# Fetching fifteen of 416 gathered edge tiles row by row from two other queues, in a graph network kernel

## The reference, cut to what matters

```
h = (x @ W).reshape(n, 8, 32)
a_src, a_dst = einsum(h, att_src), einsum(h, att_dst)        # [n, 8]
e = leaky_relu(a_src[src] + a_dst[dst], 0.2)                 # per edge and head
e = exp(e - segment_max(e, dst)[dst])
alpha = e / (segment_sum(e, dst)[dst] + 1e-16)
out = segment_sum(h[src] * alpha, dst) + bias                # then layernorm, residual, layernorm
```

## Time and profile before

| | |
|---|---|
| median of three runs | 2902.57 us |
| the profiled execution's own time | 2898.8 us |
| its span, first to last instruction | 2896.7 us |
| mean granted clock of TensorE | 0.877 |
| TensorE, matmul busy | 2220.1 us (77%) |
| VectorE busy | 1490.0 us (51%) |
| GpSimd busy | 1216.4 us (42%) |
| ScalarE busy | 663.0 us (23%) |

### The profile page before, as it was taken

How to read it: one execution, slowest core, us unless ns; L and a number is a source line. 1 busy time by engine, 2 the same in 40 slices (tenths; PEclk the granted TensorE clock), 3 DMA queues, 4 the chain that set the end, 5 groups by cost and what they waited for, 6 DMA issues and landing times.

```text
span 2896.7 us, 31032 instructions
## 1 busy us (share of the span) xinstructions
PE 2220.1 (77%) x8708; PEld 1498.8 (52%) x8708; DVE 1490.0 (51%) x4063; ACT 663.0 (23%) x1371; POOL 1216.4 (42%) x1733
## 2 busy tenths in 40 slices
PE   4677798999989869999999999999923535353550
PEld 2444798447775435655556555677712424243430
DVE  8999676556860010340105302455534757575768
ACT  3777654114540000100002000355400000000002
POOL 0000278888888800010000000001048888888850
PEclk8888999999999979999999999999956666666675
DMA  6565688443455234454445433433243333333321
GB/s 238 241 258 218 235 282 265 147 161 115 127 175 157 76 125 155 149 206 151 132 155 183 154 118 122 113 98 101 79 76 94 99 94 98 93 97 94 95 69 44
DMA packets 191911, 411.95 MB, mean 142 GB/s; under 512 B 47734, under 2 KB 131409, under 8 KB 191761
## 3 DMA queue, kind: packets, MB, share of 16 engines
q1 hardware_dynamic: 128276, 240.65, 26.3%
q10 hardware_dynamic: 27325, 102.15, 9.8%
q0 software_dynamic: 36160, 67.34, 8.5%
HBM read 326.06 MB, written 83.96 MB: 142 GB/s over the span
## 4 chain that ended last, share of the span: by engine, by line
PE 54%; POOL 18%; DVE 18%; issue 4%; DMA 4%; ACT 1%; SPq 0%; ACTq 0%; DVEq 0%; POOLq 0%
PE banks L1509 24%; POOL row_ring L2141 10%; PE banks L933 8%; DVE features_and_rows L567 6%; POOL spare_count L338 5%; PE banks L1059 4%; POOL table_dense_weights L789 4%; PE banks L1176 3%; PE banks L1191 3%; PE banks L2363 3%; DVE pair_and_bias_rows L564 2%; PE banks L1496 2%; PE banks L1949 1%; PE banks L1479 1%; PE banks L1966 1%
## 5 line engine op out<-in xcount | busy, mean ns | idle before, releaser
L789 POOL DMA_INDIRECT table_dense_weights<-pair_weight,dst x416 | 416.9, 1002 | 424.5 <-DVE weights_c L828 317.3
L1509 PE MATMUL banks<-own_term,features_and_rows 128*128 128x391 f32 (+1 forms) x1656 | 554.7, 492 | 38.4 <-DMA own_term<-table_dense_weights 38.4
L1509 PEld LDWEIGHTS banks<-own_term,features_and_rows 128*128 128x128 f32 x1656 | 313.2, 190 | 266.6 <-issue 40.9
L2141 POOL DMA_INDIRECT row_ring<-table_heads,src x416 | 408.1, 981 | 83.4 <-issue 65.6
L1535 DVE TENSOR_SCALAR features_and_rows<-banks,hop_bias 128x391 f32<-128x391 f32 (+1 forms) x24 | 15.0, 625 | 645.6 <-PE banks L1509 645.6
L933 PE MATMUL banks<-split_rows,count_columns 128*128 128x512 f32 x1200 | 310.8, 406 | 3.3 <-ACT count_columns L915 3.3
L1509 PE MATMUL banks<-features_and_rows 128*128 128x391 f32 (+1 forms) x840 | 282.4, 491 | 0.0
L338 POOL IOTA spare_count<- 128x256 int32 x728 | 263.8, 362 | 7.2
L2363 PE MATMUL banks<-row_ring,edge_to_window 128*128 x880 | 237.9, 434 | 16.9 <-DVE edge_to_window L2338 13.5
L933 PEld LDWEIGHTS banks<-split_rows,count_columns 128*128 128x128 f32 x1200 | 222.5, 189 | 53.0 <-issue 5.3
L585 PE MATMUL banks<-features_and_rows,pair_and_bias_rows 128*128 128x400 f16 x806 | 182.4, 384 | 86.9 <-DVE features_and_rows L567 52.8
(11 more groups left out here) (423 smaller groups left out, 3078.1 us busy)
## 6 DMA issues: line engine op xcount, KB each, us to landing
hidden<-table_counts SPq DMA_DIRECT2D x305, 160.0 KB
table_dense_weights<-weights_c ACTq DMA_DIRECT2D x26, 1600.0 KB, 5.7
own_term<-table_dense_weights SPq DMA_DIRECT2D x52, 782.0 KB
own_term<-table_dense_weights SPq DMA_DIRECT2D x34, 780.5 KB
pair_and_bias_rows<-table_edge_rows ACTq DMA_DIRECT2D x50, 512.0 KB
weights_c<-table_edge_rows ACTq DMA_DIRECT2D x50, 512.0 KB
features_and_rows<-table_dense_weights SPq DMA_DIRECT2D x26, 782.0 KB
table_counts<-hidden SPq DMA_DIRECT2D x25, 800.0 KB, 3.4
```

The costliest lines, as they stand in the source:

```text
L789: e.indirect_dma_start(out=self.table, out_offset=bass.IndirectOffsetOnAxis(ap=self.place[:, t:t + 1], axis=0), in_=self.values[:, t:t + 1 ...
L1509: m = e.matmul(psum[b][:, 0:wide], z_block(block)[:, f * P:(f + 1) * P], streamed[tile % STREAM][:, lo - from_column:lo - from_column + wi ...
L2141: e.indirect_dma_start(out=ring_rows[:, ring_at(t), 0:ATT_ROW], out_offset=None, in_=t_h, in_offset=bass.IndirectOffsetOnAxis(ap=src[:, t: ...
```

## The change

Fifteen tiles are taken out of `gather_rows`: the first tile of each of the parts 1 to 12 (`SYNC_TILES`), and tiles 33, 65 and 66 (`SCALAR_TILES`). Their row numbers are loaded into SBUF by fifteen small DMAs (`row_src`, one partition a tile). `load_tile_rows` then fetches such a tile with 128 DMAs of one row each: it loads 16 row numbers into registers, and for each takes a register's value as the row of `t_h`. SyncE fetches tile 32 before its loop, and in the loop, behind the start cut of part b, tile 32b (with a wait for the ring from tile 96 on, `RING_TILES` being 80). ScalarE fetches its three at the head of `merge_act`. Each of the fifteen has a semaphore of its own, for which VectorE waits with the part's quads; a quad with such a tile counts fewer landings (`gathered`). GpSimd makes no pause for a tile that it leaves out.

```diff
+SYNC_TILES = tuple(b * PART_TILES for b in range(1, PARTS))
+SCALAR_TILES = (PART_TILES + 1, 2 * PART_TILES + 1, 2 * PART_TILES + 2)
+ROW_TILES = SYNC_TILES + SCALAR_TILES
+ROW_REGS = 16
...
-        row_landed = lambda quad: (s_row[quad % RING_QUADS], 16 * GROUP * (quad // RING_QUADS + 1))
+        tiles_of = lambda quad: range(quad * GROUP, (quad + 1) * GROUP)
+        gathered = lambda quad: sum(t not in ROW_TILES for q in range(quad % RING_QUADS, quad + 1, RING_QUADS) for t in tiles_of(q))
+        row_landed = lambda quad: (s_row[quad % RING_QUADS], 16 * gathered(quad))
+        s_tile_rows = {t: pr.sem(f"tile_rows_landed{t}") for t in ROW_TILES}
+        s_row_src = pr.sem("source_rows_loaded")
+        pr.queue["sp"].append(lambda e: [e.dma_start(row_src[n:n + 1, :], a["src_run"][0:1, 1 + t * P:1 + (t + 1) * P]).then_inc(s_row_src, 16)
+                                         for n, t in enumerate(ROW_TILES)])
+
+        def load_tile_rows(e, t, regs):
+            n = ROW_TILES.index(t)
+            for p in range(P):
+                if p % ROW_REGS == 0:
+                    e.load(regs, row_src[n:n + 1, p:p + ROW_REGS])
+                node = e.snap(regs[p % ROW_REGS], min_val=0, max_val=PADDED_NODES - 1)
+                e.dma_start(ring_rows[p:p + 1, ring_at(t), 0:ATT_ROW], t_h[bass.ds(node, 1), :]).then_inc(s_tile_rows[t], 16)
...
-                for t in range(quad * GROUP, (quad + 1) * GROUP):
+                for t in tiles_of(quad):
+                    if t in ROW_TILES:
+                        continue
...
+            row_regs = [e.alloc_register(f"source_row{k}") for k in range(ROW_REGS)]
+            e.wait_ge(*w_h)
+            e.wait_ge(s_row_src, 16 * len(ROW_TILES))
+            load_tile_rows(e, SYNC_TILES[0], row_regs)
             for b in range(2, PARTS):
                 e.wait_ge(*cuts_read[b - 2])
                 load_start_cut(e, b)
+                t = SYNC_TILES[b - 1]
+                if t >= RING_TILES:
+                    e.wait_ge(*merged(t - RING_TILES))
+                load_tile_rows(e, t, row_regs)
...
+            landed += [(s_tile_rows[t], 16 * P) for t in ROW_TILES if t // PART_TILES == b]
...
         def merge_act(e):
+            row_regs = [e.alloc_register(f"scalar_source_row{k}") for k in range(ROW_REGS)]
+            e.wait_ge(*w_h)
+            e.wait_ge(s_row_src, 16 * len(ROW_TILES))
+            for t in SCALAR_TILES:
+                load_tile_rows(e, t, row_regs)
```

More of the change, by code:

```diff
@@ L210, in residual_gnn @@
         node_of = sb("node_of_tail_row", [P, 2], I32)
+        row_src = sb("source_rows", [P, P], I32)
         row_head = sb("head_of_row", [P, 1])
```

## The result

The changed kernel took 3162.59 us (median of four runs, 3160.59 to 3170.22) against 2902.39 for the kernel before (2900.96 to 2903.87): a ratio of 1.090, 95% interval 1.088 to 1.092. The profiled execution has a span of 3160.7 us, 264.0 more than before; the sum had 206.6.

What follows compares the result with a forecast made beforehand. The prediction took GpSimd's gathers and pauses to bound the attention stage. SyncE's slower row fetching would start the tail 206.6 us later: 2898.8 + 206.6 = 3105 us, 7% slower, range 2874 to 3330.

Steps and rivals of the forecast that it cites:

- the sum: Whole kernel: the profiled 2898.8 us plus 206.6 us from a later last landing, 3105 us, 7% slower.
- The row sets the landing: Attention stage: SyncE's tile of 67.7 us outlasts GpSimd's part of 46.5 us, so SyncE sets when parts land; 73%.
- the fast rival: Attention stage: SyncE keeps up, at under 380 ns a row, and 22.5 us are saved, 2876 us; chance 17%.
- The row's terms: SyncE's row: load 69, move 33, address 37, gaps 135 and DMA issue 255 ns, together 529 ns.
- the +14: SyncE's ten later tiles: forecast at 68.1 us each, they averaged 69.5.
- The first two tiles: SyncE's first two tiles: forecast at 67.7 and 68.1 us, they took 91.4 and 80.4.
- These 54 us are no term of the sum: Part 2, waiting for ScalarE: lands at 2342 instead of 2288 us, but the parts behind make it up.
- GpSimd done by 2747: GpSimd's gathers: finished by 2747 us, before SyncE's last row lands at 2976.2.
- The own rows beside the weighing: First own-rows load, issued at 2975 us: its 16 us fit beside the last part's weighing and merge, some 50 us.
- the +5.8: Tail from the last landing to the end: forecast at 127.1 us, it took 132.9.
- The price of an issue: SyncE's one-row DMA issue: taken as 255 ns, the shortest in the trace, with 430 as the other end.

Runs made afterwards that it cites:

- e3: Changed kernel, but both queues fetch fixed rows, without register loads or register operations: 2890.38 us, ratio 0.9964 to the kernel before.
- e1: Changed kernel, but ScalarE's three tiles go back to GpSimd and SyncE keeps its twelve: 3130.2 us (one run).
- e4: Changed kernel, but the 16 row numbers are loaded once a tile, not eight times, so later rows repeat the first sixteen sources: 3076.91 us (one run).
- e5: Changed kernel, but ScalarE's three tiles come from fixed rows while SyncE's twelve keep their registers: 3161.47 us (one run).
- e2: Changed kernel, but SyncE's twelve tiles go back to GpSimd and ScalarE keeps its three: 2937.79 us, ratio 1.0133 to the kernel before.
- c2: Changed kernel, but SyncE fetches only the first tile of every odd part, ScalarE none, and the first own-rows load waits for the last part's weights: 2886.21 us.
- d1: Kernel before, no tile fetched row by row, but the first own-rows load waits for the last part's weights: 2893.32 us, ratio 0.9963.

## Why the prediction was right, and where its sizes were off

**The row sets the landing: right.** The rows of a tile run through SyncE's sequencer one after the other, a tile takes longer than GpSimd's part, and each part waits for it (all but part 0, which has no such tile, and part 2, which waited for ScalarE). The chain, the landings, GpSimd's wait at the ring and VectorE's wait (169.5 us before, 368.9 + 24.9 = 393.8 now, forecast 200 more) say so, and e3 shows that the register work decides it: without it the row takes 0.30 us and SyncE keeps up, as in the fast rival, at 2890 us where the rival had 2876.

**The row's terms: the sum nearly right, its parts less so.** A row averages (69.5 - 0.4) / 128 = 0.540 us against 0.529. The load is 77 ns (1230 / 16), not 69; the move 29, not 33; the address 44, not 37; the DMA issue 225 to 228, not 255. Away from the merges the row is regular; 30 rows of the changed kernel between 2614 and 2628 us (columns as above):

```profile
L2117 SPq MOVE row_ring<-table_heads x30: 29/29/29, 2614.0 to 2627.5; - x30
L2117 SPq DMA_DIRECT2D row_ring<-table_heads x30: 227/228/269, 2614.1 to 2627.5; - x30
```

They stand 0.416 us apart where no load lies between, so that the gaps are (416 - 228 - 29 - 44) / 3 = 38 ns, not 45. With the load this is 0.496. The rest is in 11 to 25 rows of each later tile that take 0.73 to 0.84 us on average. That the average row comes so near the sum is partly luck: the regular row is 33 ns cheaper than summed, and the slow ones, for which the sum had no term, add 44. They fall into the time of a merge, as here beside the one of 2628.5 to 2648.8:

```profile
L2117 SPq MOVE row_ring<-table_heads x11: 3/14/679, 2640.1 to 2646.7; - x11
L2117 SPq DMA_DIRECT2D row_ring<-table_heads x11: 3/5/196, 2640.1 to 2647.4; - x11
```

The records read 3 to 14 ns for nearly all and 679 for one: the time lies between instructions rather than in one of them. The merge alone does not do it either. GpSimd, free of the ring, gathers from 2632.8 to 2677.8, and its last gather of all starts at 2991.0, in the merge of 2976.4 to 2995.2. Rows beside gathers and no merge, then beside gathers and a merge, then beside that merge once the gathers are over (row line, from 2650, 2985.5 and 2992.5 us on):

```profile
L2117 SPq MOVE row_ring<-table_heads x54: 3/29/29, 2650.4 to 2676.6; - x54
...
L2117 SPq MOVE row_ring<-table_heads x9: 3/14/679, 2985.8 to 2990.9; - x9
...
L2117 SPq DMA_DIRECT2D row_ring<-table_heads x5: 218/224/225, 2992.4 to 2994.1; - x5
```

The first stand 0.49 us apart with their loads, the second 0.64 on average without, and the third 0.42 again, while the merge goes on; e1, e4 and e5 show the same return at the end of the gathers. So it takes a merge and GpSimd's gathers together, as it takes ScalarE's rows and the gathers in the first two tiles. What they share stays open; 128 x 0.011 us over ten tiles are the +14.

**The first two tiles: no term.** The sum took a row of SyncE at one price whether ScalarE fetched rows or not: +36 us, the largest error. e1 takes it away (3130.2), e5 shows that the other queue's DMAs are enough for it without register work, and the stretches beside e5 that GpSimd must gather meanwhile.

**"These 54 us are no term of the sum": wrong, and hidden.** ScalarE's three tiles were done at 2364.4 and part 2 started at 2365.7. The prediction thought that the parts behind could follow faster, since it looked at VectorE's 31 us; it left out that GpSimd stands at the ring meanwhile. In e2 this costs 1.3% by itself. In the changed kernel it is no term all the same, but only because SyncE, which waited for nothing, was later still from the next part on: its tile 96, of part 3, was done at 2401, and part 3 started at 2402.0. In e5 ScalarE is done 100 us sooner, and the time is the same. For the same reason "GpSimd done by 2747" failed, its last gather starting at 2991.0; this cost nothing, the last row of SyncE landing at 3027.8:

```profile
3026.58 1.26 DMA row_ring<-table_heads
...
3036.68 1.90 DVE tmp L2338
...
3058.53 10.19 PE banks L2393 x32
```

(The chain from the last landing: start, us, what.) The landing took 1.3 us, forecast 1.4.

**The own rows beside the weighing: mis-sized.** "Fits beside the last part's weighing and merge" held for the load's time (issued at 3026.85, and GpSimd at work on it at 3036.29), but not for what GpSimd then does with it. From start to merge are 30.5 us (3028.0 to 3058.5), where the kernel before had 24.6: these are the +5.8 of the tail. The kernel before paid 8 us of this already, and c2 and d1 show it by getting down to 16.0. The Trainium skill ("SBUF — State Buffer", section "Who interferes with whom") says that VectorE and GpSimd share a pair of ports which some instructions of VectorE need, and that whichever issues first then holds it for a whole instruction while the other stands still; the trace agrees, VectorE's four operations taking 9.07 / 4 = 2.27 us each beside GpSimd's of 2.0 to 2.6. The prediction did not weigh that.

**The price of an issue.** The issue of a row on SyncE took 225 ns at the median, 252 with a fixed address (e3). The shortest issue in the trace, 255, was a good guide. The some 50 ns that the Trainium skill states for the dispatch ("DMA: Bandwidth & Descriptors", section "Anatomy of one DMA") stand there for DMAs that GpSimd issues, so the prediction set them against a row of another queue; they and the 427 estimated from the 512 cycles of the same page (section "Why a DMA increments its semaphore by 16 and not by 1") both differ from what was measured, and the measurement decides.

## What to carry to other kernels

A tile fetched row by row costs its queue 128 times the whole chain of load, register work and issue, here 69 us for 1.5 us of GpSimd; compare that sum with the interval at which the tile is due and with the time at which its place in the buffer comes free, and count what runs beside it: a second queue that does the same, a merge, and GpSimd's gathers with either. A part that comes late in a ring is not made up when the engine that sets the pace is the one that fills the ring. Ask of a load that is moved not only whether it fits, but which engine starts to work when it lands, and beside whom.

## What the runs showed of the hardware

One-row DMAs of two queues slow each other while GpSimd gathers: SyncE's tile took 68 us without ScalarE's rows, 90 beside ScalarE's rows with registers, 108 beside ScalarE's rows with fixed addresses, though each row is only 1 KB. In stretches of 24 us SyncE issued 36 rows beside ScalarE's rows and the gathers, 47 and 48 beside one of the two. A merge on TensorE and VectorE slows SyncE's rows in the same way, and again only beside the gathers. Rows with a fixed address follow each other in 0.30 us, with an address from a register in 0.42 and the load on top. VectorE's operation of 0.29 us took 1.88 beside GpSimd's multiplications.
